# Gathering eight small copies into one and widening a per-head scaling in a retention layer

## The reference

```python
Q = jnp.einsum('bld,hde->bhle', x, Wq)          # 16 heads of 64
K = jnp.einsum('bld,hde->bhle', x, Wk)
V = jnp.einsum('bld,hde->bhle', x, Wv)
scores = jnp.einsum('bhle,bhme->bhlm', Q, K) * Dm[None] / math.sqrt(HEAD_DIM)
out = jnp.einsum('bhlm,bhme->bhle', scores, V)  # Dm[l, m] = gamma_h ** (l - m), 0 above the diagonal
# group norm over (64 channels, all positions) per head, then combined @ Wout, added to x
```

## Time and profile before

| | us |
|---|---|
| profiled execution, slowest core | 6006.56 |
| its span (first to last instruction) | 6005.0 |
| spans of the 8 cores in it | 5986.8 to 6005.0 |
| runs shown, median of 2 | 6122.84 (6000.53 and 6245.15) |
| phase 1 ends, phase 2's first loads are issued | about 1209 |

### The profile page before, as it was taken

How to read it: one execution, slowest core, us unless ns; L and a number is a source line. 1 busy time by engine, 2 the same in 40 slices (tenths; PEclk the granted TensorE clock), 3 DMA queues, 4 the chain that set the end, 5 groups by cost and what they waited for, 6 DMA issues and landing times.

```text
span 6005.0 us, 65346 instructions; the slowest of 8 cores (5986.8 to 6005.0 us)
## 1 busy us (share of the span) xinstructions
PE 4990.4 (83%) x24212; PEld 2337.2 (39%) x24644; DVE 1437.5 (24%) x3601; ACT 1439.3 (24%) x3555; POOL 190.7 (3%) x333
## 2 busy tenths in 40 slices
PE   3555555559998999899989998999899989998999
PEld 1233333324443444344434443444344434443444
DVE  1444444521112111211121112111211121112111
ACT  1333333422112212221222122112212121213121
POOL 0000000000000000000000000000000000000000
PEclk9666666679998999899999998999899989998999
DMA  8777777133333343434343434333333324332423
GB/s 176 186 185 189 181 180 178 52 131 142 142 148 132 135 154 135 148 119 162 128 151 127 162 118 148 138 152 135 132 154 135 154 113 159 130 154 94 171 116 130
DMA packets 110213, 867.29 MB, mean 144 GB/s; under 512 B 11344, under 2 KB 19536, under 8 KB 75344
## 3 DMA queue, kind: packets, MB, share of 16 engines
q0 software_dynamic: 76048, 787.00, 39.1%
q1 hardware_dynamic: 33856, 76.10, 3.7%
HBM read 837.91 MB, written 103.02 MB: 157 GB/s over the span
## 4 chain that ended last, share of the span: by engine, by line
PE 69%; DMA 4%; ACT 3%; issue 2%; DVE 1%; ACTq 0%; DVEq 0%; POOL 0%; SPq 0%; POOLq 0%
PE psf L976 23%; PE psf L980 23%; PE psf L1033 21%; DMA wring<-wbf 4%; PE psf L839 2%; ACT silu_sb L992 1%; ACT xln_bf L161 1%; DMA x_sb<-x 1%; PE psb L758 1%; ACT ucp_sb L993 1%; DVE h_sb L1002 0%; DVE combT L768 0%; DVE xln2T L772 0%; ACT L151 0%; ACT sqdump L135 0%
## 5 line engine op out<-in xcount | busy, mean ns | idle before, releaser
L1033 PE MATMUL psf<-wring,h_sb 128*128 128x512 bf16 x6208 | 1451.3, 394 | 161.5 <-DVE h_sb L1002 153.1
L976 PE MATMUL psf<-xln2T,wring 128*128 128x512 bf16 x6192 | 1496.0, 381 | 20.9 <-DMA wring<-wbf 10.0
L980 PE MATMUL psf<-xln2T,wring 128*128 128x512 bf16 x6224 | 1490.5, 380 | 5.9
L992 ACT ACTIVATE silu_sb<-psf 128x512 bf16<-128x512 f32 x792 | 473.0, 597 | 3298.9 <-PE psf L980 3298.8
L1033 PEld LDWEIGHTS psf<-wring,h_sb 128*128 128x128 bf16 x6336 | 635.2, 101 | 977.6 <-issue 294.5
L1002 DVE TENSOR_TENSOR h_sb<-silu_sb,ucp_sb 128x512 bf16<-128x512 bf16 x792 | 337.0, 425 | 2442.2 <-ACT ucp_sb L993 2442.2
L976 PEld LDWEIGHTS psf<-xln2T,wring 128*128 128x128 bf16 x6336 | 620.5, 98 | 769.0 <-issue 33.0
L980 PEld LDWEIGHTS psf<-xln2T,wring 128*128 128x128 bf16 x6336 | 621.9, 98 | 754.8 <-issue 12.8
L1049 DVE SCALAR_TENSOR_TENSOR x_sb<-psf,c_sb,x_sb 128x512 f32<-128x512 f32 x576 | 432.8, 751 | 1114.9 <-PE psf L1033 1041.8
L993 ACT CAST ucp_sb<-psf 128x512 bf16<-128x512 f32 x792 | 459.5, 580 | 0.0
L254 PE MATMUL psb<-eye_sb,xln_bf 128*128 128x128 bf16 x256 | 32.3, 301 | 318.3 <-ACT xln_bf L161 312.0
(11 more groups left out here) (99 smaller groups left out, 1893.6 us busy)
## 6 DMA issues: line engine op xcount, KB each, us to landing
wring<-wbf POOLq DMA_DIRECT2D x216, 2816.0 KB, 12.2
wbf<-stg POOLq DMA_DIRECT2D x36, 1408.0 KB, 5.9
x_sb<-x SPq DMA_DIRECT2D x64, 512.0 KB, 6.6
stg<-wg POOLq DMA_DIRECT2D x16, 1408.0 KB, 10.8
stg<-wu POOLq DMA_DIRECT2D x16, 1408.0 KB, 10.7
out<-x_sb SPq DMA_DIRECT2D x32, 512.0 KB, 14.7
wbf<-stg POOLq DMA_DIRECT2D x9, 1536.0 KB, 5.8
stg<-wd POOLq DMA_DIRECT2D x8, 1536.0 KB, 12.5
```

Source lines behind the costliest of these rows:

```text
L976: t.matmul(gb, wring[:, wg0 + dt * IFF + it * C:wg0 + dt * IFF + (it + 1) * C], xln2T[:, dt * SC:(dt + 1) * SC], start=(dt == 0), stop=(dt ...
L980: ins = t.matmul(ub, wring[:, wu0 + dt * IFF + it * C:wu0 + dt * IFF + (it + 1) * C], xln2T[:, dt * SC:(dt + 1) * SC], start=(dt == 0), st ...
L992: sc.activation(silu_sb[:, (it % 2) * SC:(it % 2 + 1) * SC], gb, AF.Silu)
L1033: ins = t.matmul(db, h_sb[:, hb + it * SC + tloc * C:hb + it * SC + (tloc + 1) * C], wring[:, wd0 + it * D + dc * 512:wd0 + it * D + (dc + ...
```

## The change

Three parts. The eight pairs of copies become one pair over the whole of `qt_sb` and `kt_sb` (64 rows of 8 KB each), which SP issues after the last eviction of the group. In v2 the copy and the four multiply-and-add instructions become one multiplication of the whole 256 columns by a table `gimat`, into `octmp`, and one addition of the other product from PSUM. The table, gamma^i / 8 repeated over each head's 64 columns in f32, is loaded once in phase 0. The lists `q_evac` and `k_evac`, which only the eight pairs used, are no longer filled.

```diff
--- before.py
+++ after.py
@@ -79,6 +79,7 @@
     swd_h = nc.dram_tensor("swd", [IFF, D], F32, kind="ExternalInput")
     dmask_h = nc.dram_tensor("dmask", [C, NH * C], BF16, kind="ExternalInput").ap()
     gcols_h = nc.dram_tensor("gcols", [C, 2 * NH], F32, kind="ExternalInput").ap()
+    gimat_h = nc.dram_tensor("gimat", [C, NH * HE], F32, kind="ExternalInput").ap()
     gnwb_h = nc.dram_tensor("gnwb", [C, 16], F32, kind="ExternalInput").ap()
     eye_h = nc.dram_tensor("eye", [C, C], BF16, kind="ExternalInput").ap()
     out_h = nc.dram_tensor("out", [L, D], F32, kind="ExternalOutput").ap()
@@ -173,6 +174,8 @@
 
         dmask = sb1("dmask_sb", [C, NH * C], BF16)
         gcols = sb1("gcols_sb", [C, 2 * NH], F32)
+        gimat = sb1("gimat_sb", [C, NH * HE], F32)
+        octmp = sb1("octmp", [C, 2 * 4 * HE], F32)
         wq_bf = sb1("wq_bf", [C, 8 * D], BF16)
         wk_bf = sb1("wk_bf", [C, 8 * D], BF16)
         wv_bf = sb1("wv_bf", [C, 8 * D], BF16)
@@ -205,10 +208,11 @@
             src_t = t_main if h % 2 == 0 else t_alt
             return src_t[0:HE, (h // 2) * SC + ccx * C:(h // 2) * SC + (ccx + 1) * C]
 
-        S("sld").n += 64
+        S("sld").n += 80
 
         def p0_sync(s, tgt=S("sld").n):
-            for dst, src in ((dmask, dmask_h), (gcols, gcols_h), (gnwb, gnwb_h), (eye, eye_h)):
+            for dst, src in ((dmask, dmask_h), (gcols, gcols_h), (gnwb, gnwb_h),
+                             (eye, eye_h), (gimat, gimat_h)):
                 ins = s.dma_start(out=dst[:, :], in_=src)
                 ins.then_inc(S("sld").h, 16)
             s.wait_ge(S("sld").h, tgt)
@@ -393,26 +397,18 @@
                     ins.then_inc(S("vcq").h, 1)
                 S("vcq").n += 1
                 evac_tgts.append(("vcq", S("vcq").n))
-                if kind == "q":
-                    q_evac[idx] = ("vcq", S("vcq").n)
-                elif kind == "k":
-                    k_evac[idx] = ("vcq", S("vcq").n)
                 em("vector", vqkv)
             qkv_done_v = S("vcq").n
 
-            for et in range(8):
-                S("sld").n += 32
-
-                def qk2(s, et=et, qw=q_evac[et], kw=k_evac[et], tgt=S("sld").n):
-                    s.wait_ge(S(qw[0]).h, qw[1])
-                    s.wait_ge(S(kw[0]).h, kw[1])
-                    s.dma_start(out=qt2_sb[:, et * SC:(et + 1) * SC],
-                                in_=qt_sb[HE:2 * HE, et * SC:(et + 1) * SC]).then_inc(S("sld").h, 16)
-                    ins = s.dma_start(out=kt2_sb[:, et * SC:(et + 1) * SC],
-                                      in_=kt_sb[HE:2 * HE, et * SC:(et + 1) * SC])
-                    ins.then_inc(S("sld").h, 16)
-                    s.wait_ge(S("sld").h, tgt)
-                em("sync", qk2)
+            S("sld").n += 32
+
+            def qk2(s, qtgt=qkv_done_v, tgt=S("sld").n):
+                s.wait_ge(S("vcq").h, qtgt)
+                s.dma_start(out=qt2_sb[:, :], in_=qt_sb[HE:2 * HE, :]).then_inc(S("sld").h, 16)
+                ins = s.dma_start(out=kt2_sb[:, :], in_=kt_sb[HE:2 * HE, :])
+                ins.then_inc(S("sld").h, 16)
+                s.wait_ge(S("sld").h, tgt)
+            em("sync", qk2)
             qk2_done = S("sld").n
 
             abase = S("vca").n
@@ -534,18 +530,15 @@
                 oio_bank = bank(3 if p == 0 else 0)
                 u_bank = bank(4 if p == 0 else 1)
 
-                def v_2(v, ccx=ccx, heads=heads, oio=oio_bank, ub=u_bank,
+                def v_2(v, ccx=ccx, hg=hg, heads=heads, oio=oio_bank, ub=u_bank,
                         oir0=(m % 2) * 4 * HE, tgt=pea_p2[m]):
                     v.wait_ge(S("pea").h, tgt)
-                    v.tensor_copy(oicp[:, oir0:oir0 + 4 * HE], oio[:, 0:4 * HE])
+                    v.tensor_tensor(octmp[:, oir0:oir0 + 4 * HE],
+                                    oio[:, 256:256 + 4 * HE],
+                                    gimat[:, hg * 4 * HE:(hg + 1) * 4 * HE], ALU.mult)
                     v.drain()
-                    for hi, h in enumerate(heads):
-                        v.scalar_tensor_tensor(
-                            comb_sb[:, ccx * D + h * HE:ccx * D + (h + 1) * HE],
-                            oio[:, 256 + hi * HE:256 + (hi + 1) * HE],
-                            gcols[:, h:h + 1],
-                            oicp[:, oir0 + hi * HE:oir0 + (hi + 1) * HE],
-                            ALU.mult, ALU.add)
+                    v.tensor_add(comb_sb[:, ccx * D + hg * 4 * HE:ccx * D + (hg + 1) * 4 * HE],
+                                 octmp[:, oir0:oir0 + 4 * HE], oio[:, 0:4 * HE])
                     for hi, h in enumerate(heads):
                         tr, tc = tsl(h)
                         ins = v.scalar_tensor_tensor(tf32[tr, tc], tf32[tr, tc], gC_imm[h],
...
+    gimat = np.zeros((C, NH * HE), dtype=np.float32)
...
+        gimat[:, h * HE:(h + 1) * HE] = (g ** iota / 8.0).astype(np.float32)[:, None]
...
```

More of the change, by code:

```diff
@@ L1094, in _make_consts @@
         gcols[:, NH + h] = (g ** (C - iota)).astype(np.float32)
+        gimat[:, h * HE:(h + 1) * HE] = (g ** iota / 8.0).astype(np.float32)[:, None]
     eye = np.eye(C, dtype=ml_dtypes.bfloat16)
-    return dmask.astype(ml_dtypes.bfloat16), gcols, eye
+    return dmask.astype(ml_dtypes.bfloat16), gcols, eye, gimat
 def kernel(**inputs):
@@ L1110 @@
     gnwb = np.ascontiguousarray(np.concatenate([gnw, gnb], axis=1))
-    dmask, gcols, eye = _make_consts()
+    dmask, gcols, eye, gimat = _make_consts()
     nc = build_nc()
@@ L1117 @@
                   swd=f32("L0_ffn_sw_down"),
-                  dmask=dmask, gcols=gcols, eye=eye)
+                  dmask=dmask, gcols=gcols, eye=eye, gimat=gimat)
     in_maps = [dict(shared, x=np.ascontiguousarray(x[b])) for b in range(8)]
```

## The result

The changed kernel's profiled execution took 5914.53 us (span 5913.0) where the kernel before took 6006.56: 92.0 us less.

The account below looks back on a forecast made before the run. In phase 1 it blamed the hole of serial waited copies and the attention loop's chain through three engines. Gains of 77.5 (copies) and 28 (loop) less 2 (table) made 103.5 us off 6006.56: 5903 us, own range 5886 to 5923.

Parts of the forecast that it names:

- the hole: Phase 1, between projections and attention: 21.6 us per group with no compute engine working, TensorE waiting for K's odd heads.
- the loop: Attention in phase 1: period through VectorE, ScalarE and TensorE falls from 5.11 to 4.67 us per two blocks, gaining 28 us.
- T: Time from issue to landing of a group's 1 MB of fused copies, taken as 8.6 us, bounds 5.0 and 14.0.
- the delay of the conversions: Expert-weight conversions on POOL's queue: two more megabytes of SP's traffic beside them cost at most 10 us.
- The copies: Wait ahead of attention in phase 1 falls from 155.6 to 78.1 us over eight groups, gaining 77.5 us.
- rival 1: Phase 1's long copies are slow, as if with twice the bytes: T = 14.0, 5946 us; chance 0.20.
- the fast rival: Phase 1's copies go faster than the spill: T = 5.0 to 6.5, 5875 to 5886 us; chance 0.12.
- free ride: Eighth group of phase 1: its 1.16 us wait, after the conversions ended, rises because it comes to lie beside them.
- Rival 3: Attention loop: VectorE alone sets the pace, gaining 56 us instead of 28, 5875 us; chance 0.10.
- The table: Opening block: gimat is one more 512 KB load on SP, costing between 0 and 3.8 us, taken as 2.
- The other bound: End of phase 1: conversions set it only if attention ends 138.5 us earlier, POOL's wait at the barrier; forecast to stay off.
- The cap on all gains: Phase 1: the conversions' end limits the total gain to 128 to 138 us, 5868 to 5878 us.

Follow-up runs that it names:

- 128-partition copies: Changed kernel, conversions running, both long copies moved as 128 partitions by 4 KB instead of 64 by 8 KB; wait ahead of attention 77.3 us on cores 0 to 3.
- late cast: Changed kernel with ScalarE's cast of the state placed behind the next block's scaling of K; 5944.02 us.
- early long copies: Changed kernel with Q's long copy issued behind Q's evictions and K's behind K's, instead of both after V's; 5906.15 us.
- unwaited pairs: Kernel before, its sixteen copies kept, SP waiting once behind the last pair instead of behind each; 5882.64 us.

## Why the prediction was right, and where it was wrong

It said 5903 us with its own range of 5886 to 5923, and a gain below 2%; the executions compared here took 5907 to 5915. The mechanism was right for the hole and for the loop. Two steps failed: the size of T, and the delay of the conversions, put at 10 us at most. The sum was 103.5 us and the measured gain 92.0. By its terms:

**The copies.** Forecast 77.5 us, measured 61.7 (153.2 less 91.5). Of the 15.8 us between them 2.4 come from starting at the slowest core's 155.6 us and not at the mean; 13.4 are eight times the miss of T. The step that failed is the size of T: taken as 8.6 us from the spill, measured 10.3 (91.5 / 8 - 1.16), and 11.7 on the slowest core. What the conversions add to a long copy in the mean was priced rightly: the 128-partition copies show T = 8.5 beside them. The miss is that the spill has 128 partitions and the copy 64, which costs 2.4 us per MB bare and 1.7 beside the conversions. The prediction named that as rival 1 and left it out of the sum, since no row of before showed it. Its argument against, that a pair "shows no low rate", does not hold: of a 128 KB pair's 2.8 us those 2.4 us per MB would be 0.3. With 1.7 us added to the spill's 8.6, T = 10.3 and the sum is 90 us. That the rival's other end, T = 14.0, and the fast rival, T = 5.0 to 6.5, both missed shows in the same runs: the price with nothing beside it is 6.8 us, so 5.0 to 6.5 could not be reached at all, and T came near 14 only in single groups (14.62 less 1.16 us is 13.5) and not in the mean.

**The eighth group.** That it would lose its free ride was right: 1.16 became 14.62 us on the slowest core.

**The loop.** The period was forecast as 4.67 and is 4.67 us; the price of the two new instructions, 0.42 us each, came out to the hundredth. The term was 28 us and is 32.0: SP's wait for attention fell by 35.0 us in the mean, from 353.4 to 318.4, of which 3.0 are not the loop's, for the kernel with the copies alone changed has 350.4. Most of the 4 us on top are in each group's last block, which had been put down as 0.44 us: the offset at which the interleaved other blocks run fell as well, from 2.41 (604.69 to 607.10) to 1.97 us (561.53 to 563.50), and 8 x 0.44 is 3.5. Rival 3, VectorE alone, is refuted by the late cast: only there does VectorE set the pace, at 3.88 us.

**The table.** Forecast 2 us, measured 2.1 in the mean over the cores: the first x load left at 61.9 instead of 59.8 us. On the slowest cores the longest load of the opening block landed 2.8 us later (KB, median us from issue to landing), against the earlier trace rows:

```profile
gimat_sb<-gimat SPq DMA_DIRECT2D x1, 512.0 KB, 12.9
gate_bf<-gate POOLq DMA_DIRECT2D x1, 18.0 KB, 55.9
```

So 61.7 + 32.0 - 2.1 = 91.6 us, against 91.5 measured at the start of phase 2.

**The other bound.** This step failed too, though it cost this forecast little. The conversions were to end at most 10 us later; they ended 21.7 later in the mean, and on core 3 phase 2 already started only 7.2 us behind their last store. POOL's wait at the barrier, forecast as 30 us, is 32.0 on the slowest core, but that is chance: over the cores it is 6.6 to 32.0. The forecast of the delay counted only two megabytes new to the conversions' time. It left out that the seven megabytes of copies that had been there changed their form. In the four kernels with long copies from 64 partitions and one staging buffer the last store comes at 1096.9 to 1109.5 us in the mean, in the three with 64 KB pairs at 1075.1 to 1080.7. With the same bytes beside the conversions, the early long copies delayed them by 24 us more than the unwaited pairs did (1104.4 against 1080.7); the loop differs as well, but with waited pairs in both kernels the new loop moved the last store by only 3.8 us. The cap on all gains was given as 128 to 138 us; the early copies reached it after about 100.

What stays open is why a copy from 64 partitions slows the conversions more than its bytes do. The runs show the size of it (24.1 us on cores 0 to 3, and 11.0 with 128 partitions) and not the mechanism; nor was the early copy tried with 128 partitions.

## What to carry to other kernels

A hole that consists of waited small transfers may be the fault of the waits alone: dropping seven of eight waits gave 124 us, while fusing the transfers behind the stage that could have covered them gave 55 us (both with the old loop) and held up the neighbour. When a copy is priced by another row, the number of partitions has to agree as well as bytes and queue. And before a gain is summed up, look how far off the next bound is on every core and whether the edit itself moves it: here it came 22 us nearer, and each further gain in attention was lost until the conversions were made faster too.

## What the runs showed of the hardware

A copy of 1 MB within the on-chip memory, in two DMAs, took 6.8 us from 64 partitions and 4.4 us from 128, without the conversions; beside the conversions 10.2 and 8.5 us in the mean. The copies' median times from issue to landing in the changed kernel are these (KB, us):

```profile
qt_sb<-qt_sb SPq DMA_DIRECT2D x8, 512.0 KB, 8.0
kt_sb<-kt_sb SPq DMA_DIRECT2D x8, 512.0 KB, 11.4
```

Beside the conversions a 64 KB copy, too, took 5.1 and 5.4 us in the median in the kernel with the unwaited pairs, so an eighth of the bytes saves only a third to a half of it. In the kernel before, where each pair is waited for, the medians were 3.0 us for Q and 5.6 for K beside the conversions, and 1.9 and 2.0 in the eighth group, without them. And what a long copy pays beside the conversions depends on the moment: 13.0 us of wait in the mean when one of their loads (1280 to 1536 KB) had been issued in the 7 us before it, 9.3 when not, and 8.0 without conversions.
